# One regrouping of outputs sent from ScalarE's queue, and six slots of VectorE's table moved, in an attention block with an fp8 feed-forward

## The chip, the cores and the metric

The kernel runs on one core of a Trainium2 chip. The metric is the device time of one execution in microseconds, lower is better. TensorE does the matmuls, ScalarE (ACT) the exponentials and most copies out of PSUM, VectorE (DVE) the row maxima and the low halves of split operands, GpSimd (POOL) the causal masks and elementwise work, and SyncE (SP) issues nearly all DMAs.

## The reference

```python
xn = layernorm(x)                                # x: 16 x 512 x 256, f32
qkv = xn @ w_qkv.T + b_qkv                       # 16 heads of 16
att = q @ k.T / sqrt(16) + hope_bias             # bias depends on i - j and the head
att = softmax(where(causal, att, -inf))
out = (att @ v) @ w_proj.T + b_proj
y = (fp8(xn_bf16 / s_in) @ fp8(w / s_k)) * (s_in * s_k)
return x + out + (bf16(y) + ffn_bias)
```

## The kernel before

Every batch (16 of them, index b) is worked through in 4 groups g of 4 heads, and every group in 12 slots k. A place in the program is written (g, k). All engines have the same loop over (g, k), and tables at the top of the file (`PV_AT`, `QK_AT`, `STATS_AT` and so on) say at which place a job is put into an engine's stream. Each engine runs its stream strictly in order; semaphores tie the streams together. Batches 1 to 13 run in a hardware loop, the others are written out.

In each slot TensorE computes one tile of transposed scores (`scores_T`, tiles scoreT_a, b, c in turn) for the group at hand and one chunk of plain scores (`scores`, tiles score_a, b, c in turn) for the group two ahead. DVE takes the row maxima of that chunk (`chunk_max`), ACT takes the exponentials of the transposed tile into `probs`, POOL masks. A tile is rewritten three slots later: a chunk of scores waits for the maximum of three slots before, a transposed tile for the exponential of three slots before. `pv` multiplies the probabilities with V beside ones, so that every other row of its result is a softmax denominator.

The part around the change is the tail of a batch's attention. The `pv` of group 3 of batch b-1 stands at (0, 3) of batch b. Then:

1. `out_T` on ACT copies its PSUM bank into `OT` at (0, 4).
2. `send_attn` issues two DMAs: numerators from `OT` to `attn` (128 KB) and denominators from `OT` to `DEN` (8 KB). SP does this in `regroup`; only for the last batch does ACT.
3. `invert` on DVE takes the reciprocal of all 16 heads' denominators. It waits for the denominators of both semaphores, and stands at `INVERT_AT` = (0, 8), behind the maximum of that slot.
4. `store_recips` and `spread_recips` on SP write the inverses to DRAM and read them back, spread over partitions, into `RB` (which is `xn`).
5. `divide` on POOL in group 1, `attn_hi` on ACT at (2, 2), `attn_parts` on POOL, then the projection on TensorE from (3, 0).

Other jobs that DVE has in these slots: `QK_lo`, the low half of the next batch's q and k, at (0, 7), (0, 10), (1, 7) and (1, 10), each behind ACT's `QK_evac` of the same bank at (0, 6), (0, 9), (1, 6), (1, 9). The layernorm statistics of batch b+2 (`stats`, four, and `aggregate`, four small operations) are in group 1. The three parts of `quant_magic` for the next batch are at the start of group 2. TensorE's feed-forward job `FF` has two halves at (2, 0); the second writes the bank misc_b that QK job 3 used, so it waits for `QK_lo` of (1, 10). ACT's copies write `out_T`; TensorE's next job on that bank waits for them.

SP's stream in batch b, from its start: stacks of group 3, the row maxima of group 1 (four small DMAs, which wait for ACT's `max_T`), the regroup of group 3 of batch b-1, the load of x for batch b+2, `store_recips`, then the first stack of batch b+1 (which waits for TensorE to be through group 0 and for `QK_lo` of (0, 10)), `spread_recips`, the row maxima of group 2, and so on.

In the profile a reciprocal of DVE has the line L1013, `QK_lo` L994, `chunk_max` L1006, `stats` L976, `aggregate` L984, `quant_magic` L1029 and L1034, an exponential L928, `out_T` L901, `QK_evac` L835, the DMAs of `send_attn` L354 and L355, and FF L596.

## Time and profile before

| | |
|---|---|
| median of 3 runs | 802.25 us (798.7 to 802.85) |
| the profiled execution | 802.85 us |
| its span, first to last instruction | 801.1 us |
| busy: TensorE / DVE / ACT / POOL | 748.0 / 631.2 / 578.7 / 531.5 us |
| mean granted TensorE clock | 0.961 |
| DMA engines, busy share of q1 / q10 | 36.9% / 0.3% |
| DMAs of `send_attn` from SP / from ACT | 63 / 1 of each kind |

A line of the page or of the trace gives an engine, a source line, what is written and read, a duration, and in square brackets how long the engine had sat idle before it and who ended that. Durations of neighbours on one engine overlap a little, so the distance between two starts is what an instruction costs its engine. "SPq" and "ACTq" mark DMA-issuing instructions on those engines' own streams. The trace is periodic: between batch 2 and batch 13 the same event comes back every 45.7 us.

### The profile page before, as it was taken

The numbers are of one execution on the slowest core, as the hardware profiler recorded it, in microseconds if no ns is written. First come the engines' busy times: TensorE is split into PE (matmuls) and PEld (weight loads), VectorE is DVE, ScalarE is ACT, GpSimd is POOL, SyncE is SP. The second block draws the span as 40 slices with busy tenths as digits, with TensorE's granted clock in tenths as the row PEclk, the third lists the DMA queues.
The fourth block names the chain that finished last, engine by engine and source line by source line (L and its number), as shares of the span: only waits on it lengthen the run. The fifth ranks groups of instructions, "written<-read, shape, count | busy, mean of one in ns | idle before, by whom it ended". The sixth has DMA issues, their size and how long they took to land.

```text
span 801.1 us, 23171 instructions
## 1 busy us (share of the span) xinstructions
PE 748.0 (93%) x6313; PEld 512.3 (64%) x6313; DVE 631.2 (79%) x2395; ACT 578.7 (72%) x1258; POOL 531.5 (66%) x525
## 2 busy tenths in 40 slices
PE   6889999999999999999999999999999999999883
PEld 3556566676666766676666666666676667666552
DVE  3769888887978888887988888797888888787602
ACT  3347868778777877877786878877787787786650
POOL 6434568676776768677676767677666967757460
PEclk8859999999999999999999999999999999999886
DMA  5603333433434243333433353333424343434102
GB/s 174 237 2 141 122 124 115 174 129 130 148 146 159 104 171 121 134 134 146 167 146 122 115 178 135 127 140 146 171 105 164 115 146 122 147 142 148 44 18 86
DMA packets 55612, 106.07 MB, mean 132 GB/s; under 512 B 10528, under 2 KB 30496, under 8 KB 55584
## 3 DMA queue, kind: packets, MB, share of 16 engines
q1 hardware_dynamic: 54420, 105.05, 36.9%
q10 hardware_dynamic: 1164, 0.68, 0.3%
q8 instruction: 13, 0.21, 0.1%
q14 instruction: 15, 0.12, 0.0%
HBM read 18.68 MB, written 8.91 MB: 34 GB/s over the span
## 4 chain that ended last, share of the span: by engine, by line
PE 72%; ACT 9%; DVE 8%; issue 6%; DMA 2%; DVEq 1%; SPq 1%; POOL 1%; ACTq 0%; POOLq 0%
PE misc_a L669 14%; PE misc_a L553 13%; PE misc_b L553 10%; PE scoreT_b L643 8%; PE scoreT_a L643 5%; PE score_c L620 4%; PE score_a L620 3%; PE misc_b L669 3%; ACT probs L928 2%; PE misc_b L604 2%; ACT xnT_hi L824 2%; ACT qk_parts L835 2%; DVE row_max L1006 2%; PE scoreT_c L643 2%; PE scoreT_b L646 2%
## 5 line engine op out<-in xcount | busy, mean ns | idle before, releaser
L1204 POOL TENSOR_SCALAR_AFFINE_SELECT probs<-probs 128x512 f32<-128x512 f32 x256 | 160.1, 636 | 219.2 <-ACT probs L928 217.6
L1006 DVE CUSTOM_DVE_ANT_0 score_b<-score_b,causal_mask_q 128x384 f32<-128x384 f32 (+3 forms) x321 | 163.3, 526 | 102.8 <-PE score_b L620 102.6
L1006 DVE CUSTOM_DVE_ANT_0 score_a<-score_a,causal_mask_q 128x512 f32<-128x512 f32 x319 | 176.4, 570 | 6.4 <-PE score_a L620 3.1
L1006 DVE CUSTOM_DVE_ANT_0 score_c<-score_c,causal_mask_q 128x256 f32<-128x256 f32 (+3 forms) x384 | 172.2, 477 | 3.0 <-PE score_c L620 2.8
L928 ACT ACTIVATE probs<-scoreT_b 128x384 f32<-128x384 f32 (+1 forms) x256 | 133.8, 523 | 37.7 <-PE scoreT_b L643 16.4
L928 ACT ACTIVATE probs<-scoreT_a 128x512 f32<-128x512 f32 (+1 forms) x256 | 145.0, 566 | 7.5 <-PE scoreT_a L646 6.0
L1006 DVE DVE_READ_ACCUMULATOR2_ANT row_max<- 128x1 f32 x1024 | 146.7, 143 | 0.0
L928 ACT ACTIVATE probs<-scoreT_c 128x384 f32<-128x384 f32 (+1 forms) x256 | 135.5, 529 | 3.2 <-PE scoreT_c L646 2.7
L669 PE MATMUL misc_a<-probs,v_ones 128*32 128x128 f32 (+3 forms) x1536 | 132.3, 441 | 0.4 <-POOL probs L1204 0.4
L643 PE MATMUL scoreT_b<-stacks 64*128 64x384 f32 (+3 forms) x320 | 120.2, 395 | 2.1 <-ACT probs L928 2.0
L620 PE MATMUL score_b<-stacks 64*128 64x384 f32 (+3 forms) x321 | 118.7, 402 | 0.3 <-DVE row_max L1006 0.2
L620 PE MATMUL score_a<-stacks 64*128 64x512 f32 x319 | 109.6, 375 | 4.5 <-DVE row_max L1006 4.4
L643 PE MATMUL scoreT_c<-stacks 64*128 64x256 f32 (+3 forms) x384 | 104.6, 305 | 9.0 <-ACT probs L928 9.0
L643 PE MATMUL scoreT_a<-stacks 64*128 64x512 f32 (+3 forms) x320 | 107.6, 356 | 5.3 <-DMA low_features<-neg_max_T 2.4
L643 PEld LDWEIGHTS scoreT_b<-stacks 64*128 64x128 f32 x320 | 57.0, 185 | 68.2 <-ACT probs L928 33.1
L620 PE MATMUL score_c<-stacks 64*128 64x256 f32 (+3 forms) x384 | 98.1, 309 | 0.5 <-DVE row_max L1006 0.2
L643 PEld LDWEIGHTS scoreT_c<-stacks 64*128 64x128 f32 x384 | 68.9, 187 | 14.7 <-ACT probs L928 14.0
L669 PEld LDWEIGHTS misc_a<-probs,v_ones 128*32 128x32 f32 x1536 | 59.9, 109 | 28.7 <-issue 11.4
L620 PEld LDWEIGHTS score_c<-stacks 64*128 64x128 f32 x384 | 66.6, 189 | 5.3 <-DVE row_max L1006 5.0
L620 PEld LDWEIGHTS score_a<-stacks 64*128 64x128 f32 x319 | 55.7, 189 | 21.7 <-DVE row_max L1006 16.7
L643 PEld LDWEIGHTS scoreT_a<-stacks 64*128 64x128 f32 x320 | 57.6, 187 | 12.3 <-issue 6.7
L901 ACT ACTIVATE out_T<-misc_a 128x512 f32<-128x512 f32 x48 | 28.7, 599 | 42.6 <-PE misc_a L669 42.5
(241 smaller groups left out, 1961.2 us busy)
## 6 DMA issues: line engine op xcount, KB each, us to landing
stacks<-qk_parts SPq DMA_DIRECT2D x128, 512.0 KB, 3.7
x_ring<-in_L_attn_x SPq DMA_DIRECT2D x16, 512.0 KB, 3.4
attn<-out_T SPq DMA_DIRECT2D x63, 128.0 KB, 2.6
xn<-recips SPq DMA_DIRECT2D x31, 256.0 KB
out<-x_ring SPq DMA_DIRECT2D x15, 512.0 KB, 3.0
stacks<-neg_max_T SPq DMA_DIRECT2D x128, 4.0 KB
low_features<-neg_max_T SPq DMA_DIRECT2D x124, 4.0 KB
low_features<-probs SPq DMA_DIRECT2D x8, 128.0 KB, 4.7
```

Of the source, the lines that this page charges most:

```text
L553: last = mm(o, l(ct), r(ct), start=(ct == 0 and i == 0), stop=(ct == CT - 1 and i == 2))
L604: last = mm(bank[0:HU * 2 * TT, 0:P], MX[:, g % 2, 32 * part:32 * part + 32], ident[:, :], start=(part == 0), stop=(part == 1))
L620: last = mm(SB_[n % 3][:, o:o + w], STK[rows, u, 0, P * qt:P * qt + P], STK[rows, u, 1, 0:w], start=True, stop=True)
L643: last = mm(bank, STK[rows, u, 1, P * j:P * j + P], STK[rows, u, 0, P * j:T], start=True, stop=(g >= 2))
L646: last = mm(bank, EXT[rows, u, 1, P * j:P * j + P], EXT[rows, u, 0, P * j:T], start=False, stop=True)
L669: last = mm(bank[32 * i:32 * i + 32, P * j:T], VA[:, j, HU * g + i, :, :].rearrange("p d a -> p (d a)"), probs(g, j)[:, i, :], start=(j == ...
L824: A(XH[:, ct, :], misc_of("T", ct)[:, :], ACT.Copy).then_inc(xh_ready, 1)
L835: A(qk_part(m, 0), misc_of("QK", m)[:, :].unsqueeze(1).broadcast_to([P, 2, T]), ACT.Identity, bias=BQ[:, bias:bias + 1]).then_inc(qh_ready, 1)
L901: A(OT[:, :], misc_of("PV", g)[:, :], ACT.Copy).then_inc(ot_ready, 1)
L928: A(probs_slot(g, k), STB[(SLOTS * g + k) % 3][:, 0:w], ACT.Exp).then_inc(exp_done, 1)
L1006: last = V.tensor_tensor_reduce(bank, bank, CMQ[:, T - w:T], 1.0, LEAST, ALU.add, ALU.max, MX[:, g % 2, 8 * h + 4 + qt:8 * h + 5 + qt])
L1204: last = GP.affine_select(out=d, in_=d, compare_op=ALU.is_ge, fill=0.0, base=0, pattern=[[0, HU], [1, P]], channel_multiplier=-1)
```

## The change

Four things are changed.

- The regroup of group 3 leaves SP for every batch. ACT issues its two DMAs itself, directly behind `out_T` at (0, 4), after waiting until its own copy has been written.
- `spread_recips` moves up on SP, ahead of the first stack of batch b+1 and its waits.
- `INVERT_AT` goes from (0, 8) to (0, 6): the reciprocal stands ahead of the maximum of slot 7 and of `QK_lo` of (0, 7), where it had stood behind both.
- `STATS_AT` goes from two at (1, 3) and two at (1, 6) to one each at (1, 2), (1, 3), (1, 5) and (1, 8); `AGGR_AT` from (1, 7) to (1, 9); `MAGIC_AT` from (2, 1) to (2, 3) to (2, 0) to (2, 2).

```diff
-INVERT_AT, LAST_INVERT_AT = (0, 8), (3, 8)
-STATS_AT, AGGR_AT = [(1, 3), (1, 3), (1, 6), (1, 6)], (1, 7)
-MAGIC_AT = [(2, 1), (2, 2), (2, 3)]
+INVERT_AT, LAST_INVERT_AT = (0, 6), (3, 8)
+STATS_AT, AGGR_AT = [(1, 2), (1, 3), (1, 5), (1, 8)], (1, 9)
+MAGIC_AT = [(2, 0), (2, 1), (2, 2)]
...
                 load_max(b, 1)
-                if not first:
-                    regroup(b - 1, 3, False)
...
                     store_recips(b - 1)
+                    spread_recips(b - 1, last)
...
                     load_stack(b + 1, 0)
-                if not first:
-                    spread_recips(b - 1, last)
...
-                if g == 3 and isinstance(b, int) and b == B - 1:
-                    act.wait_ge(ot_ready, 4 * B)
+                if g == 3:
+                    act.wait_ge(ot_ready, 4 * b + 4)
                     send_attn(act, b, 3)
```

Lines of the changed file stand three lower than those of the file before from here on. No instruction is added to or taken from TensorE and POOL, and their order is the same.

ACT, group 0 of a batch in the loop, from the slot-3 exponential to that of slot 4 (out_T is the copy of the PV result). Before:

```order
L928 ACTIVATE probs<-scoreT_a 128x512 [waits scoresT_in_psum]
L846 ISA
L847 ACTIVATE neg_max_T<-misc_b 32x128 [waits max_T_in_psum]
L895 ISA
L899 ISA [waits pv_done]
L901 ACTIVATE out_T<-misc_a 128x512 [waits denominators0_regrouped,out_T0_regrouped]
L923 REGISTER_ALU
L928 ACTIVATE probs<-scoreT_b 128x384 [waits scoresT_in_psum]
```

and with the change:

```order
L925 ACTIVATE probs<-scoreT_a 128x512 [waits scoresT_in_psum]
L843 ISA
L844 ACTIVATE neg_max_T<-misc_b 32x128 [waits max_T_in_psum]
L892 ISA
L896 ISA [waits pv_done]
L898 ACTIVATE out_T<-misc_a 128x512 [waits denominators0_regrouped,out_T0_regrouped]
L354 ISA [waits out_T_written]
L354 DMA attn<-out_T 64x512
L355 DMA denominators<-out_T 32x1x64
L920 REGISTER_ALU
L925 ACTIVATE probs<-scoreT_b 128x384 [waits scoresT_in_psum]
```

A wait for the copy's own end and two DMA issues stand between the copy and the next exponential.

DVE, group 0, from the maximum of slot 6 (score_a) to that of slot 8 (score_c). Before:

```order
L1006 ISA score_a,row_max<-score_a,causal_mask_q 128x384 [waits scores_in_psum,x_loaded]
L1006 ISA score_b,row_max<-score_b,causal_mask_q 128x384 [waits scores_in_psum,x_loaded]
L994 SCALAR_TENSOR_TENSOR qk_parts<-misc_a,b_qkv,qk_parts 128x512 [waits qk_hi_written]
L1006 ISA score_c,row_max<-score_c,causal_mask_q 128x256 [waits scores_in_psum,x_loaded]
L1013 RECIPROCAL denominators_inv<-denominators 128x64 [waits denominators1_regrouped,denominators0_regrouped]
```

and with the change:

```order
L1003 ISA score_a,row_max<-score_a,causal_mask_q 128x384 [waits scores_in_psum,x_loaded]
L1010 RECIPROCAL denominators_inv<-denominators 128x64 [waits denominators1_regrouped,denominators0_regrouped]
L1003 ISA score_b,row_max<-score_b,causal_mask_q 128x384 [waits scores_in_psum,x_loaded]
L991 SCALAR_TENSOR_TENSOR qk_parts<-misc_a,b_qkv,qk_parts 128x512 [waits qk_hi_written]
L1003 ISA score_c,row_max<-score_c,causal_mask_q 128x256 [waits scores_in_psum,x_loaded]
```

(The reads of the accumulator and the register instructions between them, which are the same in both, are not shown here or below.) The reciprocal stands two maxima and one `QK_lo` earlier.

DVE, group 1, from `QK_lo` of slot 7 (misc_a) to that of slot 10 (misc_b), with the maxima of slots 8, 9 and 10 between them. Before:

```order
L994 SCALAR_TENSOR_TENSOR qk_parts<-misc_a,b_qkv,qk_parts 128x512 [waits qk_hi_written]
L984 BN_AGGR mean_var<-bn_six 128x2 [waits bn_stats_done,x_loaded]
L1006 ISA score_c,row_max<-score_c,causal_mask_q 128x256 [waits scores_in_psum,x_loaded]
L1006 ISA score_a,row_max<-score_a,causal_mask_q 128x256 [waits scores_in_psum,x_loaded]
L1006 ISA score_b,row_max<-score_b,causal_mask_q 128x256 [waits scores_in_psum,x_loaded]
L994 SCALAR_TENSOR_TENSOR qk_parts<-misc_b,b_qkv,qk_parts 128x512 [waits qk_hi_written]
```

and with the change:

```order
L991 SCALAR_TENSOR_TENSOR qk_parts<-misc_a,b_qkv,qk_parts 128x512 [waits qk_hi_written]
L1003 ISA score_c,row_max<-score_c,causal_mask_q 128x256 [waits scores_in_psum,x_loaded]
L973 BN_STATS bn_six<-x_ring 128x6
L1003 ISA score_a,row_max<-score_a,causal_mask_q 128x256 [waits scores_in_psum,x_loaded]
L981 BN_AGGR mean_var<-bn_six 128x2 [waits bn_stats_done,x_loaded]
L1003 ISA score_b,row_max<-score_b,causal_mask_q 128x256 [waits scores_in_psum,x_loaded]
L991 SCALAR_TENSOR_TENSOR qk_parts<-misc_b,b_qkv,qk_parts 128x512 [waits qk_hi_written]
```

The four `aggregate` operations (one row of four) stay between the two `QK_lo`, and one of the four `stats` has come in between them.

## Rows read from the trace of the kernel before

**Rows 1.** The page: busy time of engines, and the chain that ended last.

```profile
PE 748.0 (93%) x6313; PEld 512.3 (64%) x6313; DVE 631.2 (79%) x2395; ACT 578.7 (72%) x1258; POOL 531.5 (66%) x525
...
PE 72%; ACT 9%; DVE 8%; issue 6%; DMA 2%; DVEq 1%; SPq 1%; POOL 1%; ACTq 0%; POOLq 0%
```

**Rows 2.** Timeline of ACT, batch 8, group 0: start us, duration us, instruction, [idle before].

```profile
422.47 0.60 ACT L901 ACTIVATE out_T<-misc_a 128x512 f32<-128x512 f32 x1 [1.22 <-PE misc_a L669]
422.96 0.48 ACT L928 ACTIVATE probs<-scoreT_b 128x384 f32<-128x384 f32 x1
...
423.70 0.51 ACT L928 ACTIVATE probs<-scoreT_a 128x384 f32<-128x384 f32 x1
425.08 1.12 ACT L835 ACTIVATE qk_parts<-misc_a,b_qkv 128x1024 fp32r<-128x1024 f32 x1 [0.87 <-PE misc_a L553]
```

**Rows 3.** Timeline of ACT, end of the last batch.

```profile
782.39 0.60 ACT L901 ACTIVATE out_T<-misc_a 128x512 f32<-128x512 f32 x1 [2.33 <-PE misc_a L669]
783.02 0.59 ACTq L354 DMA_DIRECT2D attn<-out_T  x1
783.65 0.65 ACTq L355 DMA_DIRECT2D denominators<-out_T  x1
```

**Rows 4.** Timeline of DVE, batch 8, slots (0, 7) to (0, 9).

```profile
425.43 0.57 DVE L1006 CUSTOM_DVE_ANT_0 score_b<-score_b,causal_mask_q 128x384 f32<-128x384 f32 x1 [1.02 <-PE score_b L620]
...
426.23 0.75 DVE L994 SCALAR_TENSOR_TENSOR qk_parts<-misc_a,b_qkv,qk_parts 128x512 fp32r<-128x512 f32 x1 [0.18 <-ACT qk_parts L835]
426.90 0.42 DVE L1006 CUSTOM_DVE_ANT_0 score_c<-score_c,causal_mask_q 128x256 f32<-128x256 f32 x1
...
427.49 0.55 DVE L1013 RECIPROCAL denominators_inv<-denominators 128x64 f32<-128x64 f32 x1
427.95 0.41 DVE L1006 CUSTOM_DVE_ANT_0 score_a<-score_a,causal_mask_q 128x256 f32<-128x256 f32 x1
```

**Rows 5.** Timeline of TensorE's weight loads (PEld), batch 8; lines with a wait.

```profile
428.72 0.18 PEld L620 LDWEIGHTS score_a<-stacks 64*128 64x128 f32 x1 [0.23 <-DVE row_max L1006]
...
431.25 0.18 PEld L620 LDWEIGHTS score_a<-stacks 64*128 64x128 f32 x1 [0.34 <-DVE row_max L1006]
```

**Rows 6.** Timeline of SP, batch 8, and an issue in the last batch.

```profile
425.03 0.61 SPq L355 DMA_DIRECT2D denominators<-out_T  x1
426.12 0.41 SPq L371 DMA_DIRECT2D x_ring<-in_L_attn_x  x1
...
776.51 0.57 SPq L355 DMA_DIRECT2D denominators<-out_T  x1
```

**Rows 7.** Timeline of DVE: the two reciprocals of the last batch.

```profile
778.64 0.55 DVE L1128 RECIPROCAL denominators_inv<-denominators 96x64 f32<-96x64 f32 x1 [0.28 <-DMA denominators<-out_T]
786.93 0.55 DVE L1145 RECIPROCAL denominators_inv<-denominators 32x64 f32<-32x64 f32 x1 [7.74 <-DMA denominators<-out_T]
```

**Rows 8.** DMA engines from 780 to 790 us, GB/s in 40 slices of 0.25 us.

```profile
GB/s 92 6 0 0 0 0 0 0 74 90 131 205 205 172 107 98 90 328 262 74 82 82 57 41 25 8 0 0 0 0 0 0 0 33 0 0 0 0 0 0
```

**Rows 9.** Timeline of TensorE, batch 8, group 0.

```profile
425.47 0.33 PE L643 MATMUL scoreT_a<-stacks 64*128 64x256 f32 x1
```

**Rows 10.** Timeline of DVE, batch 8, group 1 and the start of group 2.

```profile
433.00 0.75 DVE L976 BATCH_NORM_STATS2 bn_six<-x_ring 128x6 f32 x2
434.20 0.57 DVE L1006 CUSTOM_DVE_ANT_0 score_b<-score_b,causal_mask_q 128x384 f32<-128x384 f32 x1 [0.45 <-PE score_b L620]
...
437.53 0.75 DVE L994 SCALAR_TENSOR_TENSOR qk_parts<-misc_a,b_qkv,qk_parts 128x512 fp32r<-128x512 f32 x1
438.20 0.37 DVE L984 BATCH_NORM_AGGREGATE mean_var<-bn_six 128x2 f32<-128x6 f32 x4
...
440.37 0.75 DVE L994 SCALAR_TENSOR_TENSOR qk_parts<-misc_b,b_qkv,qk_parts 128x512 fp32r<-128x512 f32 x1
```

**Rows 11.** Waits of TensorE's weight loads: total us, times, longest us.

```profile
PEld misc_b L596 <- DVE qk_parts L994: 7.2, 15, 0.6
```

**Rows 12.** Timeline of weight loads, group 2: the wait after the moved `quant_magic`.

```profile
446.54 0.19 PEld L553 LDWEIGHTS misc_a<-w_qkvT_hi,xnT_hi 128*128 128x128 f32 x1 [0.47 <-ACT out_T L901]
```

## The prediction

> **What bounds the kernel now.** I read the busy times first, then the chain that ended last, then one batch of the loop engine by engine. TensorE is busy 93% of the span and makes up 72% of the chain [rows 1]; ACT and DVE come into the chain for short pieces between matmuls. So the time is TensorE's in-order stream plus the places where it waits. A change off TensorE pays only if it shortens such a wait, and costs if it makes one. A batch of the loop takes 45.7 us.
>
> In group 0 of batch 8 I want the reader to see this. ACT copies out_T at 422.47 and goes on at once; it then has 0.87 us of idle time before it copies the first QK bank at 425.08 [rows 2]. DVE has idled 1.02 us before the maximum of slot 7, since 424.41 (425.43 less 1.02), and from 426.23 works without a gap: QK_lo 0.67 to the next start, maximum of slot 8 0.59, reciprocal 0.46, maximum of slot 9 from 427.95 [rows 4]. TensorE waits for this string twice, 0.23 before the scores at 428.72 (the maximum of slot 9 gives back their tile) and 0.34 before those at 431.25 [rows 5]. The reciprocal's 0.46 us is thus on a path that TensorE feels, and taking it out of there is where the change could gain.
>
> In group 1, QK_lo of slot 7 starts at 437.53 and QK_lo of slot 10 at 440.37, with aggregate and three maxima between them [rows 10]; the second half of FF waits for the later one in 15 batches, 7.2 us of idle weight loads in all [rows 11]. Two stats at 433.00 take 0.75 and are followed by 0.45 us of idle DVE, so there they cost nothing [rows 10]; the pair at (1, 6) has a like gap behind it.
>
> **The two DMAs on ACT.** Where ACT does this today, in the last batch, out_T starts at 782.39, the numerators are issued at 783.02 and the denominators at 783.65, until 784.30 [rows 3]. So ACT is free 1.91 us after the start of the copy, against 0.49 in the loop (422.96 less 422.47) [rows 2]. The exponential of slot 4 moves from 422.96 to about 424.4, that is 1.4 later. Three exponentials take 0.37 each, so the QK copy starts at about 425.55 instead of 425.08: 0.87 of the 1.4 lie in the idle time and 0.5 is left. On TensorE, the transposed tile of slot 6 is given back at 424.4 + 0.74 + 0.51 = about 425.7, and slot 9 wanted it at 425.47 [rows 9]. I take **0.25 us** per batch on TensorE. Its bounds are 0 (if the two issues overlap the exponentials) and 0.5 (all that is left over of the QK copy). Behind ACT's wait stand the exponentials, behind those TensorE and POOL's masks; the masks are wanted only at (1, 3).
>
> **The reciprocal at (0, 6).** ACT issues the denominators 1.26 us after out_T starts [rows 3], so at 423.73; SP issued them at 425.03 [rows 6]. The reciprocal now comes up at 424.41, and the data cannot be there: it waits, and with it the maximum of slot 7, QK_lo, and all behind them. How long is the open quantity. From SP, in the last batch, the issue at 776.51 [rows 6] was waited for until 778.64 [rows 7], 2.13 us; in the loop the data was there at 427.49, at most 2.46 us after the issue at 425.03 [rows 4, 6]. From ACT, the issue at 783.65 [rows 3] was waited for until 786.93 [rows 7], 3.28 us.
>
> I take 2.2. The one ACT-issued transfer ran while the DMA engines carried 74 to 328 GB/s of other work from 784 us to 786.25 [rows 8] (the inverses being spread), and in the loop SP has only small row-maximum DMAs there. The Trainium skill (DMA: Bandwidth & Descriptors, Issuing engines are not separate DMA queues) says that DMAs started from either engine run on the same 16 DMA engines and that a second issuer saves only issue time. By that rule both take 2.13 and the sum below is right; by the row of 3.28 the sum is that of the second rival.
>
> Then: data at 425.93, reciprocal 0.46, maximum of slot 7 at 426.4, 0.63 long with its read, QK_lo at 427.05 instead of 426.23. (ACT's QK copy ends at 425.55 + 1.12 = 426.7, so it isn't the later.) That is 0.82 later, but the 0.46 of the reciprocal is gone behind it: the string runs 0.36 later than before, and TensorE at 428.72 loses some 0.3 of it, since its score reads had a little slack. This runs beside the 0.25 from ACT, not on top of it. Group 0 together: **0.3 us**, bounds 0.25 and 1.4 (3.28 instead of 2.13 adds 1.15 to the string). 15 batches have it: 15 x 0.3 = **4.5 us**, bounds 4 and 21.
>
> **Stats, aggregate, magic.** QK_lo of (1, 7) is started by ACT as before. Between it and QK_lo of (1, 10) stood one aggregate (0.31 to the next start) and three maxima; now one of the stats stands there too, 0.75 / 2 = 0.37, and it has about 0.33 between starts in the middle of a string. DVE comes to QK_lo of (1, 10) without any idle time before it, with ACT's copy only just done, so nothing of this is hidden behind ACT: QK_lo starts 0.33 later and the second half of FF too. 14 batches have stats: 14 x 0.33 = **4.6 us**. Bounds: 0 (if the waits between aggregate's operations now hide under a maximum better than they did) and 14 x 0.67 = 9 (if aggregate's own waits, until now under QK_lo's 0.75, come into the open and cost as much as it and the stat). The other three stats go into slots of group 1 whose idle time covers them; if it didn't, TensorE still has two slots before it wants those maxima. quant_magic one slot earlier puts off the maxima of slots 1 to 3 of group 2 by up to 0.6; TensorE wants the last of them in slot 6 and then waits 0.47 for out_T anyway [rows 12]. Cost 0, at most 0.15 x 15 = 2.
>
> **SP.** It loses two issues of 0.6 and gets the load of x out some 1.9 us earlier (it went at 426.12 [rows 6]); spread_recips comes before the first stack. The gain to TensorE is 0: x is read in group 1, the stack in group 2, the divided outputs in group 2, all with microseconds to spare, and in the loop no wait of TensorE is for a DMA. The earlier load of x can collide with the denominators: at worst that is the late landing of the second rival.
>
> **Sum.** Against the profiled execution, 802.85 (span 801.1 and 1.75 around it): 4.5 + 4.6 = 9.1, so 812.0 us; that execution stands 0.6 above the median of 802.25. I say **811.5 us**, 1.1% slower. Taking the bounds of the two terms, 802.85 + 4 + 0 = 807 to 802.85 + 9 + 9 = 821 if the landing is no more than 2.5.
>
> **Rivals.**
> 1. *Nothing to measure.* The delays are taken up by other waits: ACT's two issues lie in its idle time, the stat in slot 8 is hidden by QK_lo waiting for ACT, and the reciprocal's 0.46 leaves the string. For it: ACT had 0.87 idle, DVE 1.02. Against: both start before the data can land. 15 x 0.2 at most, 802 to 806. I take 804.
> 2. *The landing from ACT is late.* For it: the only ACT-issued instance, 3.28 us. Against: the DMA engines were busy then. Group 0 costs 15 x 1.4 = 21, with the stat 4.6: 828.
> 3. *Faster.* The mechanism is the string that TensorE waits for at 428.72 and 431.25. If the denominators are there by 424.97 (425.43 less 0.46), the reciprocal runs wholly in idle time and 0.46 us leaves the string: 15 x 0.46 = 6.9 less, 796. It decides at a landing of 1.24 us after ACT's issue, with ACT's copy of QK not late. Against: the same kind of DMA took 2.13 at the least. If the stat costs its 4.6 as well, the time is 800.5.
> 4. *The change doesn't do what it says:* ACT's wait for its own copy costs more than in the last batch since its pipeline is full. It adds to the 0.25 only, and ends within the forecast's range.
>
> **How the numbers follow.** Forecast (807 to 821) 0.45; rival 2 and what lies between it and the forecast (821 to 830) 0.17; rival 1 (798.5 to 806.5) 0.22; rival 3 (under 798.2) 0.16. The range takes the forecast, rival 1 and half of rival 2: 798 to 826 leaves 0.16 below and 0.05 above, about 2 in 10. A difference within 0.5% (4 us) of 802.25 can't be told from no change. Slower by more than that: 0.45 + 0.17 = 0.62 and a little of rival 1, 0.64. Within: 0.20. Faster: 0.16.
>
> **What would show it.** In the profile after: the exponential behind out_T in group 0 starts about 1.9 us after it (0.5 before); the reciprocal has an idle time of about 1.5 us before it, ended by the DMA of the denominators, 15 times, and its start less ACT's issue is the landing, 2.2 by the forecast, 3.3 by rival 2, under 1.3 by rival 3; the maximum of slot 7 starts 0.5 us or less behind the reciprocal and no longer on TensorE's release; the second half of FF waits 0.3 us more for QK_lo; the loop's period is 46.3 us. If the period is 45.7 or less I am wrong, and the first thing to look at is whether the two idle times were larger than I read; if the DVE waits are as said and the period still doesn't grow, the string wasn't on TensorE's path.

## The result and the profile after

| | median, us | runs | profiled execution, us | its span, us |
|---|---|---|---|---|
| before | 800.48 (798.53 to 802.85) | 4 | 802.85 | 801.1 |
| after | 811.53 (809.94 to 812.63) | 4 | 810.14 | 808.4 |

The ratio of after to before is 1.0135, with a 95% interval of 1.0095 to 1.0175: the change costs 1.4%. In the traces one batch of the loop, from one reciprocal to the next, took 45.69 us before ((610.20 - 336.09) / 6) and takes 46.33 after ((616.95 - 338.98) / 6). The difference is 0.60 to 0.71 us in each of the twelve batches between; 14 times 0.64 are 9.0 us.

The busy times and the chain of the page of after, to be held against [rows 1]:

```profile
PE 752.4 (93%) x6313; PEld 515.3 (64%) x6313; DVE 624.6 (77%) x2395; ACT 578.6 (72%) x1258; POOL 531.1 (66%) x525
PE 69%; ACT 7%; DVE 7%; issue 6%; DMA 6%; SPq 3%; ACTq 1%; DVEq 1%; POOL 0%; POOLq 0%
```

No engine has more instructions of any weight to run. What has grown in the chain is DMA (2% to 6%), SPq (1% to 3%) and ACTq (0% to 1%), the time in which ACT issues DMAs. ACT around out_T of group 0 in batch 7 of after (start, duration, engine, line, operation, tiles, and in brackets the idle time before it and what ended it; line numbers are 3 lower than before):

```profile
381.61 0.60 ACT L898 ACTIVATE out_T<-misc_a 128x512 f32<-128x512 f32 x1 [1.22 <-PE misc_a L666]
382.37 0.57 ACTq L354 DMA_DIRECT2D attn<-out_T  x1
382.98 0.56 ACTq L355 DMA_DIRECT2D denominators<-out_T  x1
383.66 0.49 ACT L925 ACTIVATE probs<-scoreT_b 128x384 f32<-128x384 f32 x1 [1.45 <-issue]
...
384.79 1.13 ACT L832 ACTIVATE qk_parts<-misc_a,b_qkv 128x1024 fp32r<-128x1024 f32 x1
```

The exponential starts 2.05 us after out_T (383.66 less 381.61), where it was 0.49 in [rows 2], and the copy of the first QK bank has lost its idle time. It starts 3.18 us after out_T instead of 2.61.

DVE in the same place, to be held against [rows 4]:

```profile
383.42 0.14 DVE L1003 DVE_READ_ACCUMULATOR2_ANT row_max<- 128x1 f32 x1
385.30 0.55 DVE L1010 RECIPROCAL denominators_inv<-denominators 128x64 f32<-128x64 f32 x1 [1.74 <-DMA denominators<-out_T]
385.77 0.54 DVE L1003 CUSTOM_DVE_ANT_0 score_b<-score_b,causal_mask_q 128x384 f32<-128x384 f32 x1
386.23 0.14 DVE L1003 DVE_READ_ACCUMULATOR2_ANT row_max<- 128x1 f32 x1
386.23 0.75 DVE L991 SCALAR_TENSOR_TENSOR qk_parts<-misc_a,b_qkv,qk_parts 128x512 fp32r<-128x512 f32 x1
```

The denominators were issued at 382.98 and the reciprocal, which waited for them, started at 385.30: counted in this way they landed 2.32 us after ACT's issue. The maximum of slot 7, ready for its turn, stood behind that wait; it starts 4.16 us after out_T instead of 2.96 (425.43 less 422.47).

Weight loads of TensorE in batch 7, of slot 7, of the scores of (1, 0) and (1, 3), and of the second half of FF, to be held against [rows 5] and, for the last, the wait of [rows 11]:

```profile
384.20 0.18 PEld L640 LDWEIGHTS scoreT_b<-stacks 64*128 64x128 f32 x1 [0.59 <-ACT probs L925]
...
388.30 0.18 PEld L617 LDWEIGHTS score_a<-stacks 64*128 64x128 f32 x1 [0.22 <-DVE row_max L1003]
...
400.96 0.33 PEld L593 LDWEIGHTS misc_b<-ffn_w_q,xq 128*128 128x128 bf16 x4 [0.72 <-DVE qk_parts L991]
```

The bracket at (1, 0) reads 0.22 where it read 0.23, as if nothing had happened; the load itself comes 6.69 us after out_T instead of 6.26. A wait in the middle of a row of engines that wait for one another keeps its size and moves. So the tables below compare distances from the start of group 0's out_T, and not the brackets.

The same in the waits of the whole kernel (total us, times, longest), two lines of after:

```profile
DVE denominators_inv L1010 <- DMA denominators<-out_T: 26.4, 15, 2.0
PEld misc_b L593 <- DVE qk_parts L991: 10.5, 15, 0.7
```

15 waits of 1.76 us that were not there, and 10.5 us where [rows 11] had 7.2, that is 0.22 more per batch.

### The profile page after: what moved, and what is told of

The parts are those of the page before. It is cut to its first block, busy times and chain, and to the rows that moved or that the text cites. A ratio compares the mean times of both kernels' runs of the same rounds, so it can differ in the third digit from the quotient of the medians.

```text
span 808.4 us, 23158 instructions
## 1 busy us (share of the span) xinstructions
PE 752.4 (93%) x6313; PEld 515.3 (64%) x6313; DVE 624.6 (77%) x2395; ACT 578.6 (72%) x1258; POOL 531.1 (66%) x525
## 4 chain that ended last, share of the span: by engine, by line
PE 69%; ACT 7%; DVE 7%; issue 6%; DMA 6%; SPq 3%; ACTq 1%; DVEq 1%; POOL 0%; POOLq 0%
PE misc_a L666 13%; PE misc_a L550 10%; PE misc_b L550 10%; PE scoreT_b L640 8%; PE scoreT_a L640 5%; PE score_a L617 4%; PE score_c L617 4%; DMA x_ring<-in_L_attn_x 4%; PE misc_b L666 3%; SPq L341 3%; ACT probs L925 3%; PE misc_b L601 2%; ACT xnT_hi L821 2%; PE scoreT_c L640 2%; DVE row_max L1003 1%
## 5 line engine op out<-in xcount | busy, mean ns | idle before, releaser
L640 PE MATMUL scoreT_c<-stacks 64*128 64x256 f32 (+3 forms) x384 | 106.6, 309 | 8.9 <-ACT probs L925 8.9
```

Source lines behind the costliest of these rows:

```text
L640: last = mm(bank, STK[rows, u, 1, P * j:P * j + P], STK[rows, u, 0, P * j:T], start=True, stop=(g >= 2))
```

## The experiments

For each kernel I give the median, the ratio to the kernel before on the same chip with its interval, and the loop's period in its trace, the mean of the same six batches as above. In before, after, tail_only, tables_only and stats_only each of the first twelve batches differs from this mean by under 0.1 us and most by under 0.03, so the periods tell apart what the medians can't. The periods of the others vary more, by 0.1 us in no_stat_in_8 and denominators_first and by over 1 where the stalls are long. The distances, in us from the start of out_T of group 0 to five weight loads of TensorE in batch 7 ("no wait": the load at (1, 0) doesn't wait for DVE):

| kernel | slot 7 | slot 10 | (1, 0) | (1, 3) | FF, 2nd half | period |
|---|---|---|---|---|---|---|
| before | 2.37 | 5.15 | 6.26 | 8.79 | 18.72 | 45.69 |
| after | 2.59 | 5.55 | 6.69 | 9.23 | 19.35 | 46.33 |
| tail_only | 2.58 | 5.55 | 6.68 | 9.21 | 19.14 | 46.12 |
| tables_only | 2.37 | 5.15 | 6.26 | 8.79 | 18.90 | 45.89 |
| act_send_reciprocal_8 | 2.58 | 5.56 | 6.82 | 9.35 | 19.27 | 46.25 |
| reciprocal_6_only | 2.36 | 5.14 | 7.85 | 10.38 | 20.30 | 47.3 |
| denominators_first | 2.59 | 5.55 | no wait | 8.95 | 19.13 | 46.11 |
| no_stat_in_8 | 2.37 | 5.15 | 6.25 | 8.78 | 18.64 | 45.83 |
| magic_only | 2.37 | 5.15 | 6.26 | 8.79 | 18.70 | 45.92 |
| stats_only | 2.36 | 5.14 | 6.24 | 8.77 | 18.90 | 45.90 |
| reciprocal_late | 2.37 | 5.14 | no wait | 8.50 | 18.51 | 49.1 |
| act_send_late | 2.59 | 5.56 | no wait | 8.95 | 18.94 | 49.6 |

**The change in two halves.** tail_only has ACT's DMAs, the earlier reciprocal and SP's new order, with stats, aggregate and quant_magic as before:

```
-INVERT_AT, LAST_INVERT_AT = (0, 8), (3, 8)
+INVERT_AT, LAST_INVERT_AT = (0, 6), (3, 8)
...
+                    spread_recips(b - 1, last)
...
+                if g == 3:
+                    act.wait_ge(ot_ready, 4 * b + 4)
                     send_attn(act, b, 3)
```

> Only the first half of the change: ACT sends group 3, the inverses are spread earlier, reciprocal at (0, 6); the tables of stats, aggregate and quant_magic as before. The loop's period was 45.67 us before and 46.3 after. In the trace of after, TensorE's weight load at (1, 3) stands 9.23 us behind the start of out_T, against 8.78 before, and the second half of FF 19.35 against 18.70. Theory (two separate costs, about 0.42 in group 0 and 0.24 at FF): period 46.1, time 5 to 7 us over before. Rival (the whole loss is the group 0 part, and the stat would have cost nothing without it): period 46.3, 9 us. Rival (FF alone): 45.7, no difference.

806.99 us (7 runs), ratio 1.0058 [1.0040, 1.0076], period 46.12: 0.43 more than before. All of it is there by (1, 0) and none is added later.

tables_only has the other half alone:

```
-STATS_AT, AGGR_AT = [(1, 3), (1, 3), (1, 6), (1, 6)], (1, 7)
-MAGIC_AT = [(2, 1), (2, 2), (2, 3)]
+STATS_AT, AGGR_AT = [(1, 2), (1, 3), (1, 5), (1, 8)], (1, 9)
+MAGIC_AT = [(2, 0), (2, 1), (2, 2)]
```

> Only the moved stats, aggregate and quant_magic; sending, spreading and reciprocal as before. Theory of two separate costs: FF's second half waits 0.24 us more for QK_lo of (1, 10), period 45.9, 3 to 4 us over before. By the prediction's own term 0.33: 46.0 and 4.6 us. Rival (the stat in slot 8 is hidden): 45.67, no difference.

805.72 us (10 runs), ratio 1.0030 [1.0012, 1.0048], period 45.89: 0.20 more, which appears at the second half of FF (18.72 to 18.90). The halves add: 0.43 + 0.20 = 0.63, and the whole change has 0.64.

**The tail taken apart.** act_send_reciprocal_8 is tail_only with the reciprocal back at (0, 8):

```
-INVERT_AT, LAST_INVERT_AT = (0, 6), (3, 8)
+INVERT_AT, LAST_INVERT_AT = (0, 8), (3, 8)
```

> As the first kernel, but the reciprocal stays at (0, 8), where it finds its data. Theory 1 (ACT's two issues hold back the exponentials and the QK copy by 0.4 to 0.5 us, and that alone is the cost of group 0): period as in the first kernel, 46.1, since QK_lo starts 0.5 later with ACT's copy and the reciprocal is back in the string with 0.46. Theory 2 (the reciprocal's wait for its data is the cost): the wait is gone, period back to 45.7 to 45.8.

810.42 us (4 runs), ratio 1.0092 [1.0060, 1.0124], period 46.25: 0.56 more than before. Theory 2 has fallen, and theory 1 was 0.15 short. DVE and TensorE in its batch 7:

```profile
386.58 0.75 DVE L991 SCALAR_TENSOR_TENSOR qk_parts<-misc_a,b_qkv,qk_parts 128x512 fp32r<-128x512 f32 x1 [0.46 <-ACT qk_parts L832]
...
387.84 0.55 DVE L1010 RECIPROCAL denominators_inv<-denominators 128x64 f32<-128x64 f32 x1
...
389.07 0.18 PEld L617 LDWEIGHTS score_a<-stacks 64*128 64x128 f32 x1 [0.38 <-DVE row_max L1003]
```

The reciprocal waits for nothing here, and still this costs more than tail_only. QK_lo now waits 0.46 us for ACT's late copy of QK, and the reciprocal's 0.46 stands behind it. So with ACT issuing the DMAs the move of the reciprocal to (0, 6) is a small gain (46.25 to 46.12), though it waits 1.74 us there. What ACT does is enough for a cost of this size, without any wait for the landing. (This kernel and tail_only also have spread_recips earlier on SP; no run has that alone.)

reciprocal_6_only is the kernel before with the reciprocal at (0, 6) and the DMAs still on SP:

```
-INVERT_AT, LAST_INVERT_AT = (0, 8), (3, 8)
+INVERT_AT, LAST_INVERT_AT = (0, 6), (3, 8)
```

> The kernel before with the reciprocal at (0, 6) and nothing else: SP sends group 3 as before, its denominators are issued 2.56 us behind the start of out_T and land 2.1 to 2.3 later. ACT holds nothing back. If the string of DVE is on TensorE's path: the reciprocal starts at 427.2 in batch 8's terms instead of idling from 424.4, QK_lo at 428.3 instead of 426.2, less the 0.46 that leaves the string: period up by 1.2 to 1.6, 47.0, 820 to 825 us. If DVE's string has room: under 0.5 more, below 810.

832.91 us (4 runs), ratio 1.0372 [1.0331, 1.0414]. The reciprocal waits 2.88 us, and (1, 0) comes 1.59 us later; so the wait that ACT's earlier issue shortens by 1.1 us is worth 1.2 us of TensorE. This much was expected. But the median is 31 us up, 2.1 a batch, and above the 820 to 825 that was expected. The batches aren't alike: of the first twelve in the trace seven take 47.24 to 47.31 and five 48.5 to 48.8, and from the second on every third is a long one. In one of the five, the stretches behind the wait (us from the start; TensorE's busy time and instructions, its granted clock as a share of full speed, share of the DMA engines, GB/s):

```profile
443.00:444.00 1.00, 0.89 (x4) 1.00 0.59 137
444.00:445.00 1.00, 0.61 (x6) 1.00 1.07 381
445.00:446.00 1.00, 0.44 (x6) 1.00 0.17 39
446.00:447.00 1.00, 1.00 (x10) 0.65 0.00 0
447.00:448.00 1.00, 1.00 (x8) 0.50 0.00 0
448.00:449.00 1.00, 1.00 (x6) 0.50 0.34 127
449.00:450.00 1.00, 1.00 (x8) 0.64 1.00 369
450.00:451.00 1.00, 0.82 (x7) 1.00 1.01 381
```

TensorE was busy for 0.89, 0.61 and 0.44 of three microseconds, and then its granted clock was 0.5, that is 1.2 GHz instead of 2.4, for most of four. The shortfall of these four adds up to 1.7 us (0.35 + 0.50 + 0.50 + 0.36), and these batches are 1.5 longer. In batch 7, one of the short ones, the stall is the same and the clock stays up:

```profile
396.00:397.00 1.00, 0.59 (x3) 1.00 0.73 242
397.00:398.00 1.00, 0.61 (x6) 1.00 0.89 294
398.00:399.00 1.00, 0.72 (x8) 1.00 0.01 3
399.00:400.00 1.00, 1.00 (x10) 1.00 0.00 0
```

In after, where (1, 0) is only 0.43 late, the granted clock is 1.00 in every 5 us between 150 and 640 us, as it is in before. The Trainium skill (TensorE: Matmul & The Clock Gate, Part 1: The HAM clock gate) describes a gate that passes part of the clock's pulses according to how busy TensorE has been. The fall behind an underused stretch agrees with that in kind; why two batches of three keep their clock through the same stall is not shown here.

**The order of the two DMAs.** denominators_first is the changed kernel with the denominators issued ahead of the numerators:

```
-            eng.dma_start(attn_row(b)[r:r + HU * HD, g // 2, :], OT[0:P:2, :]).then_inc(ot_stored[g % 2], 16)
             eng.dma_start(DEN[32 * g:32 * g + 32, :], OT[1:P:2 * HD, :]).then_inc(den_loaded[g % 2], 16)
+            eng.dma_start(attn_row(b)[r:r + HU * HD, g // 2, :], OT[0:P:2, :]).then_inc(ot_stored[g % 2], 16)
```

> The changed kernel with the two DMAs of a regroup in the other order, denominators first: they are issued 0.6 us earlier and should land about 0.6 earlier, so the reciprocal waits 1.1 instead of 1.74. ACT is held as long as before. Theory 1 (ACT's hold bounds group 0, TensorE is already late at slot 7 and slot 10): period stays at 46.3. Theory 2 (the landing bounds it): period 0.2 to 0.4 lower, 3 to 6 us less than after.

807.30 us (7 runs), ratio 1.0071 [1.0039, 1.0102], period 46.11: 0.22 less than after, as in theory 2. Its ACT queue and DVE in batch 7:

```profile
380.50 0.57 ACTq L354 DMA_DIRECT2D denominators<-out_T  x1
...
382.34 0.56 DVE L1010 RECIPROCAL denominators_inv<-denominators 128x64 f32<-128x64 f32 x1 [0.52 <-DMA denominators<-out_T]
383.13 0.57 DVE L1003 CUSTOM_DVE_ANT_0 score_b<-score_b,causal_mask_q 128x384 f32<-128x384 f32 x1 [0.24 <-PE score_b L617]
...
384.21 0.75 DVE L991 SCALAR_TENSOR_TENSOR qk_parts<-misc_a,b_qkv,qk_parts 128x512 fp32r<-128x512 f32 x1 [0.45 <-ACT qk_parts L832]
```

The reciprocal now runs in DVE's idle time, and the maximum of slot 7 waits for TensorE as before. ACT's hold is untouched (slot 10 still comes 0.40 late) and shows as QK_lo's wait of 0.45 for the copy. Since the reciprocal's 0.46 is gone behind it, TensorE is only 0.16 late at (1, 3), against 0.44 in after. So in after the landing sets the end of group 0, and ACT's hold lies under it; take the landing away and ACT's hold is next, smaller by 0.22 a batch. (The order is turned in every group's regroup here; the rows shown are those of group 3.)

**Stats and quant_magic apart.** no_stat_in_8 is tables_only with the fourth stat at (1, 5) instead of (1, 8):

```
-STATS_AT, AGGR_AT = [(1, 2), (1, 3), (1, 5), (1, 8)], (1, 9)
+STATS_AT, AGGR_AT = [(1, 2), (1, 3), (1, 5), (1, 5)], (1, 9)
```

> The moved tables alone, as in tables_only (period 45.89), but the fourth of the stats at (1, 5) instead of (1, 8); aggregate at (1, 9) and quant_magic at (2, 0) to (2, 2) stay moved. Theory (the stat between the two QK_lo is the whole cost): period 45.69 as before. Rival (aggregate's own waits or quant_magic cost part of it): 45.75 to 45.89.

805.12 us (10 runs), ratio 1.0056 [1.0032, 1.0079], period 45.83. FF comes at 18.64, earlier than before, although aggregate has moved: the stat in slot 8 was the 0.2 there. Yet the period hardly falls, since TensorE now waits at the scores of (2, 6):

```profile
401.86 0.18 PEld L620 LDWEIGHTS score_a<-stacks 64*128 64x128 f32 x1 [0.34 <-DVE row_max L1006]
```

That is the place of quant_magic, which I had costed at nothing. Two more kernels, each with one of the table changes alone, test it. magic_only:

```
-MAGIC_AT = [(2, 1), (2, 2), (2, 3)]
+MAGIC_AT = [(2, 0), (2, 1), (2, 2)]
```

> The kernel before with quant_magic one slot earlier and nothing else. In no_stat_in_8 FF was not late, but the scores of (2, 6) waited 0.34 us for a maximum of DVE, and the V job stood 0.17 us later than before. If quant_magic's place is the cause: period 45.83, as there (45.69 before), with the same wait at (2, 6). By the prediction's term (at most 0.15, taken as 0): 45.69. Rival (aggregate at (1, 9) is the cause): 45.69 and no such wait.

804.00 us (10 runs), ratio 1.0014 [0.9994, 1.0033]: the median doesn't tell it from no change. In its trace four batches in a row (2 to 5) and the 13th take 45.53 to 45.69 us, no more than before, and the eight others 45.85 to 46.05. The V job's load in slot 6 of group 2 is released by out_T in the first kind. In the second the scores ahead of it wait for the maximum, and the load comes 0.2 to 0.4 later (here 24.31 us after out_T of group 0, in the first kind 24.07):

```profile
310.37 0.19 PEld L553 LDWEIGHTS misc_a<-w_qkvT_hi,xnT_hi 128*128 128x128 f32 x1 [0.26 <-ACT out_T L901]
...
355.92 0.18 PEld L620 LDWEIGHTS score_a<-stacks 64*128 64x128 f32 x1 [0.34 <-DVE row_max L1006]
356.28 0.19 PEld L553 LDWEIGHTS misc_a<-w_qkvT_hi,xnT_hi 128*128 128x128 f32 x1 [0.18 <-issue]
```

What makes the difference stands on DVE and GpSimd a few us earlier, first kind and second kind:

```profile
305.00 1.23 POOL L1204 TENSOR_SCALAR_AFFINE_SELECT probs<-probs 128x512 f32<-128x512 f32 x2
306.09 0.69 DVE L1029 TENSOR_SCALAR xn<-quant_work 128x1024 int32<-128x1024 int32 x1
...
350.99 1.24 POOL L1204 TENSOR_SCALAR_AFFINE_SELECT probs<-probs 128x512 f32<-128x512 f32 x2
351.77 1.00 DVE L1029 TENSOR_SCALAR xn<-quant_work 128x1024 int32<-128x1024 int32 x1
```

L1029 is the first of quant_magic's three parts. Where it starts 0.14 us before the end of GpSimd's pair of masks, it takes 0.69; where it starts 0.46 before, it takes 1.00. So it is in every batch of magic_only: 0.69 or 0.70 in the five short ones, 0.96 to 1.07 in the eight others. In no_stat_in_8 it takes 0.84 to 1.09 in all thirteen, and the batch with 0.84 is the shortest of them (45.71). So what the earlier place costs is this meeting with GpSimd's masks; where they don't meet, the place costs nothing. This is read from the 26 batches of two traces, and no run moves the masks alone. Why the masks come 0.3 us later in some batches is not shown either. stats_only:

```
-STATS_AT, AGGR_AT = [(1, 3), (1, 3), (1, 6), (1, 6)], (1, 7)
+STATS_AT, AGGR_AT = [(1, 2), (1, 3), (1, 5), (1, 8)], (1, 9)
```

> The kernel before with stats and aggregate moved and quant_magic left at (2, 1) to (2, 3). tables_only had a period of 45.89 and magic_only, without the stat in slot 8, 45.92, so either move alone may give all of the 0.2. The prediction's term (the stat between the two QK_lo costs, quant_magic doesn't): period 45.9, FF's second half 0.2 late. Rival (the stat costs nothing by itself, quant_magic all): 45.69. Both costs real but overlapping, since TensorE runs 0.2 later at FF and so no longer meets the late maximum of (2, 3): 45.9 here as well, with no wait at (2, 6).

806.77 us (5 runs), ratio 1.0057 [1.0036, 1.0078], period 45.90, with FF 0.18 later and no wait at (2, 6). So the third theory had the numbers right: stats alone costs 0.2 us, quant_magic alone 0.2 in eight batches of thirteen, and both together 0.20. The rows give a plainer reason than the overlap of two waits. With the stat in slot 8, DVE comes to L1029 20.00 us after out_T instead of 19.79, and in tables_only it takes 0.69 to 0.85, in after 0.69 or 0.70 in all thirteen: the masks are over or nearly so.

**Two tries to separate ACT's hold from the landing.** reciprocal_late moves the reciprocal of the kernel before to (1, 0) and, to keep SP from waiting for it, the spreading of the inverses behind the row maxima of group 2. act_send_late has the same and the DMAs on ACT:

```
-INVERT_AT, LAST_INVERT_AT = (0, 8), (3, 8)
+INVERT_AT, LAST_INVERT_AT = (1, 0), (3, 8)
...
+                load_max(b, 2)
                 if not first:
                     spread_recips(b - 1, last)
-                load_max(b, 2)
```

> The kernel before with the reciprocal at (1, 0) instead of (0, 8), behind the maxima that TensorE waits for, and spread_recips on SP behind the row maxima of group 2 instead of before them; SP sends as before. If the reciprocal's 0.46 us is on TensorE's path in the string of DVE: the waits in front of the scores of (1, 0) and (1, 3) shrink, period 45.69 down to 45.3 to 45.5, 3 to 6 us faster than before. Rival (ACT's QK copy and TensorE's own work bound this stretch and DVE follows): period as before, 45.7. If the divided outputs come too late for attn_hi at (2, 2): slower.

> ACT sends group 3 as in after, but the reciprocal stands at (1, 0), where it neither waits nor stands in the string; spread_recips behind the row maxima of group 2; tables of group 1 and 2 as before. What is left of group 0's cost is ACT's hold alone. Theory 1 (ACT's two issues and its wait are the cost, 0.4 us): period 46.0 to 46.1, as with the reciprocal at (0, 6) (46.12). Theory 2 (the late start of DVE's string is the cost): period at or below 45.7.

856.83 us (4 runs), ratio 1.0709 [1.0648, 1.0771], and 859.51 us (4 runs), ratio 1.0730 [1.0686, 1.0775]. Both are over 50 us slower than before, for a reason of their own. Of reciprocal_late:

```profile
POOL attn L1238 <- DMA attn<-out_T: 64.5, 13, 5.7
PEld misc_a L669 <- POOL probs L1204: 52.1, 16, 4.2
```

POOL's division waits both for attn and for the inverses. The row names attn, but the numerators of group 3 were issued at 402.10 in batch 7 and the division starts at 420.34; the inverses were issued at 414.55, that is 14.4 us after out_T instead of 8.95 in before. So it is the inverses that come late, and behind the division stand POOL's masks, for which TensorE waits 3.3 us a batch. The times and periods of the two kernels therefore say nothing on ACT's hold.

The distances of the table do. Group 0 is over before the division, and in reciprocal_late slots 7 and 10 stand where they do in before. With the reciprocal out of the string, TensorE is at (1, 3) after 8.50 us instead of 8.79, and with ACT's hold added after 8.95. So ACT's hold alone, with no landing waited for and no reciprocal in the string, puts TensorE back by 0.45 there and by 0.43 at FF. In denominators_first, where the reciprocal runs in idle time, (1, 3) comes at the same 8.95. In after it comes at 9.23, 0.73 above the 8.50: the larger of the two delays shows, and the smaller isn't added to it. The pair also shows that the spreading of the inverses has a due time after all.

**The reciprocal alone, later.** The same move with SP's order as before (reciprocal_1_0):

```
-INVERT_AT, LAST_INVERT_AT = (0, 8), (3, 8)
+INVERT_AT, LAST_INVERT_AT = (1, 0), (3, 8)
```

> The kernel before with the reciprocal at (1, 0) and nothing else: SP's order is that of before, so the inverses are spread as soon as they are stored, about 3.5 us sooner than with the spreading behind the row maxima (reciprocal_late, where GpSimd's divide waited 4.2 us in every batch). If the lateness of the spreading was the whole loss there, and the reciprocal is in TensorE's path at (0, 8): the loop's period is 45.4 to 45.6 against 45.69, 2 to 4 us faster than before. If divide still waits or the row maxima of group 2 now land too late for TensorE at (2, 0): slower, by up to 1 us per batch.

830.05 us (820.52 to 834.74, 4 runs), ratio 1.0355 [1.0314, 1.0397]: slower by more than the 1 us per batch that was allowed for. And with the storing of the inverses behind the first stack on SP (reciprocal_1_0_stack):

```
-                if not first:
-                    store_recips(b - 1)
 
                 if not last:
...
                     load_stack(b + 1, 0)
                 if not first:
+                    store_recips(b - 1)
```

> As reciprocal_1_0, with SP's storing of the inverses behind the first stack of the next batch, so that the stack isn't held by the wait for the later reciprocal. If SP's queue is what is short of time: 0.1 to 0.5 us per batch better than reciprocal_1_0. If not: the same.

806.90 us (800.44 to 810.67, 10 runs), ratio 1.0046 [1.0018, 1.0073]: 23 us less, where 0.1 to 0.5 per batch were expected. TensorE's waits for the row maxima, of reciprocal_1_0 (in its quickest execution, 820.52 us) and then of reciprocal_1_0_stack:

```profile
PE scoreT_a L643 <- DMA stacks<-neg_max_T: 22.6, 16, 2.1
```

```profile
PE scoreT_a L643 <- DMA stacks<-neg_max_T: 12.5, 16, 1.4
```

In both the wait of [rows 5] at (1, 0) is gone: with the reciprocal out of the string, TensorE is at (1, 3) 0.3 us earlier (8.50 and 8.51 instead of 8.79). But SP waits for the reciprocal before it stores the inverses, and the row maxima of group 2 are queued behind that on SP. The kernel before has one such wait in all, 1.2 us. The gain is real and is paid for elsewhere; no kernel here beat the one before.

## Why the prediction held, point by point

The forecast was 811.5 us; 811.53 was measured. The period was forecast at 46.3 and is 46.33. The period is what was predicted, though two of its terms are right only in their sum. That the total agrees to 0.03 us is luck: the forecast was 9.25 above a median of 802.25, and the measured difference is 11.05 above a median of 800.48. And the stated range, 798 to 826, held the forecast, rival 1 and half of rival 2; it is the waits and the period that speak for the forecast and against the others.

- **What bounds the kernel.** Right. Nothing but waits changed, and each 0.1 us of TensorE per batch is in the time: 0.64 x 14 = 9.0 us, against 11.05 between the medians and 7.3 between the two profiled executions. The rest lies outside the loop: from the first reciprocal of the last batch to its second there are 32.93 us before and 31.33 after, from the reciprocal of batch 14 to that of batch 15 44.28 and 45.67. No run explains these.
- **ACT's hold.** That it costs is right, the size was low, and the path was not the one I priced. I took 1.91 us from out_T to the exponential; it is 2.05, and slot 10 comes 0.40 late where I had 0.25, within the bounds of 0 to 0.5. I priced it through the transposed tiles alone. Its larger price is QK_lo, which waits 0.46 for ACT's copy as soon as the reciprocal isn't holding it: 0.45 at (1, 3) by itself (act_send_late against reciprocal_late, where the load at (1, 3) waits for DVE in both), and 0.56 a batch in act_send_reciprocal_8. It didn't hurt the sum, because the landing covers it.
- **That the two run side by side.** Right: over the 8.50 of reciprocal_late the hold alone gives 0.45 at (1, 3), and both together give 0.73, which is the landing's: in after ACT's copy of QK ends at 385.92 (384.79 and 1.13), and QK_lo starts at 386.23, straight behind the maximum. Taking the landing away brings the hold out (denominators_first, 8.95).
- **The landing.** Taken at 2.2, measured 2.32 in batch 7 (2.28 to 2.35 in the middle batches); rival 2 (3.28 us, 828 us) fell. The slow instance in [rows 3, 7, 8] belongs to its place: the last landing takes 2.71 to 3.32 us in all fourteen kernels. Whether the busy DMA engines make it so isn't shown. My reading of [rows 8] was off as well: 74 to 328 GB/s were carried only until 785.5 us, behind that 57 down to 8. The Trainium skill (DMA: Bandwidth & Descriptors, Issuing engines are not separate DMA queues) says that all issuing engines' DMAs run on the same 16 DMA engines, and the traces agree as far as they go: in reciprocal_6_only the landing from SP was 2.27, from the issue at 393.63 to the reciprocal at 395.90. The same section calls the sequencer's time for an issue usually small beside the DMA. Here it is 0.57 beside 2.32, and what costs is that ACT's next exponential stands behind two of them and a wait.
- **The string of DVE.** I had TensorE 0.3 later; it is 0.43. The landing was 0.12 longer than taken, and I had allowed for a little slack in front of the scores at (1, 0), which isn't there: the load at (1, 0) still waits 0.22 for the string, so whatever the string is late, TensorE is late. This term is 0.13 x 15 = 2.0 us too low.
- **The stat in slot 8.** Right in place, too high in size: 0.33 against 0.20. QK_lo of slot 7 to QK_lo of slot 10 was 2.84 us in [rows 10] and is 3.04 in after (400.16 less 397.12). The rows below show where the missing 0.13 is. This term is 0.13 x 14 = 1.8 us too high, which makes up for the one above.
- **quant_magic at no cost.** Right as far as the wait for out_T in [rows 12] goes, which covered it in the five short batches of magic_only. What I had not seen is that in the earlier place its first part can meet GpSimd's masks and take 1.00 us instead of 0.69. In the change itself it doesn't meet them, since the stat in slot 8 has put DVE back by 0.2. So the zero in the sum is right partly by luck.
- **SP.** Right that it gives TensorE nothing: after has no wait of TensorE for a DMA in the loop, and the halves add up without a term for it. The load of x goes out 1.55 us earlier and not 1.9 (2.11 us after out_T, 3.66 before). No run has SP's part alone.
- **Rivals 1 and 3** needed the waits to be hidden or a landing under 1.24 us; 2.32 rules out the second, and the offsets at (1, 0) and FF the first. Rival 3 had also priced the gain too high: with the reciprocal out of the string TensorE is only 0.29 earlier at (1, 3) and 0.21 at FF (8.50 and 18.51 in reciprocal_late), not 0.46. Rival 4 is the 0.14 us by which the exponential is later than in the last batch. It was of no weight, as said.

DVE in group 1 of after, where the stat stands, to be held against [rows 10]:

```profile
397.12 0.75 DVE L991 SCALAR_TENSOR_TENSOR qk_parts<-misc_a,b_qkv,qk_parts 128x512 fp32r<-128x512 f32 x1
...
398.38 0.42 DVE L973 BATCH_NORM_STATS2 bn_six<-x_ring 128x6 f32 x1
398.71 0.41 DVE L1003 CUSTOM_DVE_ANT_0 score_a<-score_a,causal_mask_q 128x256 f32<-128x256 f32 x1
...
399.29 0.37 DVE L981 BATCH_NORM_AGGREGATE mean_var<-bn_six 128x2 f32<-128x6 f32 x4
399.59 0.41 DVE L1003 CUSTOM_DVE_ANT_0 score_b<-score_b,causal_mask_q 128x256 f32<-128x256 f32 x1
...
400.16 0.75 DVE L991 SCALAR_TENSOR_TENSOR qk_parts<-misc_b,b_qkv,qk_parts 128x512 fp32r<-128x512 f32 x1
```

And two maxima of the same size in before, which stand right behind the read of the maximum ahead of them:

```profile
439.11 0.47 DVE L1006 CUSTOM_DVE_ANT_0 score_a<-score_a,causal_mask_q 128x256 f32<-128x256 f32 x1
...
439.74 0.47 DVE L1006 CUSTOM_DVE_ANT_0 score_b<-score_b,causal_mask_q 128x256 f32<-128x256 f32 x1
```

The stat takes 0.33 to the next start and the aggregate 0.30, about as I had them. But a maximum that follows one of these instead of a read takes 0.41 and not 0.47. Two of them are shorter by 0.06, 0.12 in all, and 0.33 - 0.12 = 0.21. Why a maximum is longer behind a read isn't shown. Here small work put between two operations cost less than its own time.

## What to carry to other kernels

A DMA issued from a computing engine isn't free on that engine: here two issues and a wait put 1.6 us in front of the next exponential, and an engine that is 72% busy had 0.9 us to spare for it in that place. When two late things meet in one string of waits, price each alone and look which ends last; taking away the one that shows brings out the other. Compare distances from a common event, since a wait's length can stay the same while all of it moves. They also keep an experiment useful whose total is spoilt elsewhere, as in the pair at 857 and 860 us. And before an instruction is moved to where its engine has room, look at what the other engines do there.

## What the runs showed of the hardware

- Where DVE's string held TensorE up for about 1.6 us, its granted clock fell to half for some 3 us in one batch of three, and that cost another 1.5 us; in the other batches the same stall left it at 1.00 (reciprocal_6_only). Where TensorE was 0.4 us late it stayed at 1.00 (after, 150 to 640 us). A wait that is four times as long can cost more than four times as much.
- DVE's `TENSOR_SCALAR` on 128x1024 int32 (L1029) took 0.69 us, and up to 1.09 when it started while a mask of GpSimd ran. By GpSimd's spans, which are rough, it then ended 0.55 us behind the end of the mask: started 0.29 before that end it took 0.84, 0.46 before it 1.00, 0.54 before it 1.09 (magic_only, no_stat_in_8).
- The place of a small DMA in its queue shows in its landing. The denominators landed 2.32 us after their issue with the numerators ahead of them, and 1.84 us (382.34 less 380.50) with nothing ahead of them in ACT's queue. At the end of the last batch it took 2.71 to 3.32 us in every kernel.
- The issue of a DMA took ACT 0.57 and 0.56 us; from the start of out_T's 0.60 us copy to the next exponential there were 2.05 us, in which ACT computed for 0.60 (after, batch 7).
